# Counting tokens per expert on TensorE straight from the comparison, with the running total on GpSimd and, in the last three steps, on VectorE

## The reference

```python
_, top_group_idx = jax.lax.top_k(group_scores, n_top_groups)        # 4 of 8 groups
top_scores, top_idx = jax.lax.top_k(masked, K)                      # K = 4 of 32 experts
capacity = max(1, int(N / E * K * CAP_FACTOR))                      # 640 slots per expert
onehot = jax.nn.one_hot(flat_e, E, dtype=jnp.int32)
pos = jnp.cumsum(onehot, axis=0)[jnp.arange(N * K), flat_e] - 1     # place in the expert's queue
keep = pos < capacity
buf = jnp.zeros((E + 1, capacity, d), xf.dtype).at[e_s, p_s].set(xf[tok])[:E]
```

## Time and profile before

| | us |
|---|---|
| three runs | 600.43, 603.52, 605.98 |
| median | 603.52 |
| profiled execution, its time | 604.68 |
| its span in the profile | 602.5 |

### The profile page before, as it was taken

How to read it: one execution, slowest core, us unless ns; L and a number is a source line. 1 busy time by engine, 2 the same in 40 slices (tenths; PEclk the granted TensorE clock), 3 DMA queues, 4 the chain that set the end, 5 groups by cost and what they waited for, 6 DMA issues and landing times.

```text
span 602.5 us, 20827 instructions
## 1 busy us (share of the span) xinstructions
PE 513.2 (85%) x7427; PEld 423.3 (70%) x7427; DVE 424.7 (70%) x1297; ACT 323.1 (54%) x832; POOL 343.0 (57%) x362
## 2 busy tenths in 40 slices
PE   3558997989988798887669889999989999999756
PEld 2336665766666566665545589999989999998544
DVE  5666799779999899966676366756666676664264
ACT  3336775767777677655546225455446555454200
POOL 8520113276666566655777507777777777777600
PEclk9659998989999999977899979999999999999977
DMA  7889998887877665520000134543534554541198
GB/s 254 234 234 249 250 248 235 225 268 212 240 231 208 210 209 151 137 66 25 21 12 10 36 99 140 150 123 108 164 119 140 171 155 149 170 118 49 24 394 292
DMA packets 79417, 98.33 MB, mean 163 GB/s; under 512 B 12097, under 2 KB 59999, under 8 KB 79216
## 3 DMA queue, kind: packets, MB, share of 16 engines
q1 hardware_dynamic: 65280, 82.92, 47.2%
q0 software_dynamic: 9216, 12.02, 6.4%
q10 hardware_dynamic: 4848, 2.40, 1.4%
HBM read 50.00 MB, written 54.30 MB: 173 GB/s over the span
## 4 chain that ended last, share of the span: by engine, by line
PE 38%; DVE 6%; DMA 5%; issue 4%; POOL 3%; ACT 2%; SPq 0%; POOLq 0%; DVEq 0%; ACTq 0%
PE banks L1115 18%; PE banks L1141 12%; DMA rload<-pair_results 3%; PE banks L1126 3%; POOL expert_slots L490 2%; DVE mx L1239 1%; PE banks L932 1%; DMA pair_results<-yout,yidx 1%; PE banks L1050 1%; POOL pair_results L618 1%; PE banks L1167 0%; DMA xg<-expert_slots 0%; SPq L440 0%; PE banks L874 0%; ACT yout L805 0%
## 5 line engine op out<-in xcount | busy, mean ns | idle before, releaser
L618 POOL DMA_INDIRECT pair_results<-yout,yidx x160 | 159.3, 996 | 67.0 <-issue 38.1
L490 POOL DMA_INDIRECT expert_slots<-xfe,sidx x128 | 127.8, 998 | 89.7 <-issue 38.9
L1115 PE MATMUL banks<-xgT_parts,wgu_parts 128*128 128x320 f32 x768 | 131.3, 320 | 1.9 <-DVE hact L1506 1.7
L1115 PEld LDWEIGHTS banks<-xgT_parts,wgu_parts 128*128 128x128 f32 x768 | 113.9, 190 | 4.6 <-DVE hact L1506 2.3
L1239 DVE TENSOR_REDUCE mx<-banks 128x8 f32<-128x1024 f32 x64 | 78.0, 1219 | 21.0 <-PE banks L882 21.0
L1506 DVE TENSOR_TENSOR hact<-hact,banks 128x320 f32<-128x320 f32 x128 | 56.6, 482 | 43.0 <-ACT hact L786 42.1
L805 ACT ACTIVATE yout<-banks,ypair 128x128 f32<-128x128 f32 x160 | 44.8, 372 | 76.2 <-PE banks L1141 73.8
L655 ACT ACTIVATE pt<-banks 128x512 f32<-128x512 f32 x128 | 69.3, 593 | 27.9 <-PE banks L913 26.6
L1141 PE MATMUL banks<-wdn,hact 128*128 128x128 f32 x640 | 76.6, 275 | 1.1 <-DVE hact L1506 1.1
L1141 PEld LDWEIGHTS banks<-wdn,hact 128*128 128x128 f32 x640 | 75.0, 192 | 1.3 <-issue 1.3
L786 ACT ACTIVATE hact<-banks 128x320 f32<-128x320 f32 x128 | 53.5, 452 | 33.1 <-PE banks L1115 31.4
(11 more groups left out here) (154 smaller groups left out, 945.5 us busy)
## 6 DMA issues: line engine op xcount, KB each, us to landing
expert_slots<-xg SPq DMA_DIRECT2D x32, 325.0 KB, 4.8
xg<-expert_slots SPq DMA_DIRECT2D x32, 325.0 KB
pair_results<-zero SPq DMA_DIRECT2D x32, 256.0 KB
rload<-pair_results SPq DMA_DIRECT2D x16, 512.0 KB, 8.9
kS<-rotated_keys SPq DMA_DIRECT2D x32, 240.0 KB
qS<-rotated_queries SPq DMA_DIRECT2D x32, 192.0 KB
wgu<-in_L_ffn_wg_dram SPq DMA_DIRECT2D x32, 128.0 KB
wgu<-in_L_ffn_wu_dram SPq DMA_DIRECT2D x32, 128.0 KB
```

The costliest lines, as they stand in the source:

```text
L490: g.indirect_dma_start(out=slots_d, out_offset=bass.IndirectOffsetOnAxis(ap=sidx[:, m % NB, j, k:k + 1], axis=0), in_=xfe[:, m % NB, j, k, ...
L618: g.indirect_dma_start(out=pairs_d, out_offset=bass.IndirectOffsetOnAxis(ap=yidx[:, c, j:j + 1], axis=0), in_=yout[:, c, j, :], in_offset= ...
L1115: last = mm(bank[2 + 2 * w + h][:, 0:CH], wgu_parts[:, e.b, wp, w, h * P:(h + 1) * P], xgT_parts[:, e.b, xp, ch * CH:(ch + 1) * CH], start ...
```

## The change

`oh` becomes bf16, and PE takes it as it stands: one product with `before_b` per choice (four), the product with the running total, and one with `ones_b` per choice for tile 0 (four): nine products for three. DVE's reduce L1387 goes. PE and POOL now wait for the comparison itself (`route`, 16 r + 16). POOL's `counted()` makes the sum over choices and tiles from `oh` in three adds (128, 64 and 32 numbers per partition) and then adds the total, so four instructions for two. For the last three windows (LAST = 3, r = 13, 14, 15; steps without p) POOL does nothing of this, and DVE does it with a reduce and an add right behind the comparison. Since `oh` has one buffer that PE and POOL now read too, DVE's comparison waits until the products of window r - 1 are done (`pos_done`) and POOL's first add of window r - 1 is (`marks_added`).

```diff
@@ tiles
-        oh = sb("oh", [P, 2, TOPK, NE])
+        oh = sb("oh", [P, 2, TOPK, NE], BF16)
+        oh2 = sb("oh2", [P, TOPK, NE])
+        oh3 = sb("oh3", [P, 2, NE])
-        marks = sb("marks", [P, 2, 3, NE], BF16)
+        sofar = sb("sofar", [P, 2, NE], BF16)
@@ GpSimd
                 def counted():
-                    pool.wait_ge(S.sel_ready, r + 1)
+                    pool.wait_ge(S.route, 16 * r + 16)
...
-                    g.tensor_tensor(sum2[:, :], m[:, 1], m[:, 2], ALU.add).then_inc(S.marks_added, 1)
-                    pool.wait_ge(S.marks_added, r + 1)
+                    g.tensor_tensor(oh2[:, :, :], oh[:, 0], oh[:, 1], ALU.add).then_inc(S.marks_added, 1)
+                    pool.wait_ge(S.marks_added, 3 * r + 1)
+                    g.tensor_tensor(oh3[:, :, :], oh2[:, 0:2], oh2[:, 2:TOPK], ALU.add).then_inc(S.marks_added, 1)
+                    pool.wait_ge(S.marks_added, 3 * r + 2)
+                    g.tensor_tensor(sum2[:, :], oh3[:, 0], oh3[:, 1], ALU.add).then_inc(S.marks_added, 1)
+                    pool.wait_ge(S.marks_added, 3 * r + 3)
                     wait(pool, S.pos_done, r)
-                    g.tensor_tensor(marks[:, 1 - r % 2, 0], m[:, 0], sum2[:, :], ALU.add).then_inc(S.acc_ready, 1)
+                    g.tensor_tensor(sofar[:, 1 - r % 2], sofar[:, r % 2], sum2[:, :], ALU.add).then_inc(S.acc_ready, 1)
@@ GpSimd, steps without p
                     dispatch(z, 1, 1)
-                    if r is not None:
-                        counted()
                     for k in range(2, TOPK):
@@ TensorE
-                    pe.wait_ge(S.sel_ready, z + 1)
+                    pe.wait_ge(S.route, 16 * z + 16)
...
-                    mm(both, before_b[:, :], m[:, 1:3], start=True, stop=False, skip_group_check=True)
-                    mm(both, ones_b[:, :], m[:, 0:1].broadcast_to([P, 2, NE]), start=False, stop=False,
+                    for k in range(TOPK):
+                        mm(both, before_b[:, :], oh[:, :, k], start=(k == 0), stop=False, skip_group_check=True)
+                    mm(both, ones_b[:, :], sofar[:, z % 2].unsqueeze(1).broadcast_to([P, 2, NE]), start=False, stop=False,
                        skip_group_check=True)
-                    mm(both[:, 1], ones_b[:, :], m[:, 1], start=False, stop=True, skip_group_check=True)\
-                      .then_inc(S.pos_done, 1)
+                    for k in range(TOPK):
+                        last = mm(both[:, 1], ones_b[:, :], oh[:, 0, k], start=False, stop=(k == TOPK - 1),
+                                  skip_group_check=True)
+                    last.then_inc(S.pos_done, 1)
@@ VectorE
                 def mark():
                     dve.wait_ge(S.route, 16 * r + 14)
+                    wait(dve, S.pos_done, r)
+                    wait(dve, S.marks_added, 3 * r - 2 if r <= NP - LAST else 0)
...
+                def counted():
                     dve.wait_ge(S.route, 16 * r + 16)
-                    wait(dve, S.pos_done, r - 1)
-                    wait(dve, S.acc_ready, r - 1)
-                    with nc.allow_low_precision("zeros and ones"):
-                        v.tensor_reduce(marks[:, r % 2, 1:3], oh[:, :, :, :].rearrange("p j k e -> p j e k"), AX.X,
-                                        ALU.add).then_inc(S.sel_ready, 1)
+                    dve.wait_ge(S.acc_ready, r)
+                    v.tensor_reduce(sum2[:, :], oh[:, :, :, :].rearrange("p j k e -> p e (j k)"), AX.X, ALU.add)\
+                     .then_inc(S.marks_added, 1)
+                    dve.wait_ge(S.marks_added, 3 * (NP - LAST) + (r - NP + LAST + 1))
+                    wait(dve, S.pos_done, r)
+                    v.tensor_tensor(sofar[:, 1 - r % 2], sofar[:, r % 2], sum2[:, :], ALU.add).then_inc(S.acc_ready, 1)
...
                 at(r, mark)
+                if r is not None and p is None:
+                    counted()
```

5 lines of the change are left out of this document (2 added, 3 removed).

## The result

| | runs | median us | lowest to highest |
|---|---|---|---|
| before | 12 | 602.19 | 598.65 to 609.32 |
| changed | 12 | 598.05 | 590.75 to 602.14 |

The ratio is 0.9886, 95% interval 0.9849 to 0.9923, a gain of 1.1%. All ratios in this document leave out slow runs, those over 1.5% above the fastest run of their kernel (five of the changed kernel's twelve), while the medians of the table are of all runs and stand only 0.7% apart. The forecast was 597.0 us, worked out from a median before of 603.52 us; over twelve runs the median before is 602.19, so the two medians differ by 4.1 us where the forecast had 6.5.

The account below looks back on a forecast made before the run. DVE was taken to set the full steps and POOL's queue the experts' start. The terms, -4.6 + 0.9 - 0.6 - 2.3 = -6.6 us, gave 597.0 us from a median of 603.52, range 593.0 to 602.0.

Parts of the forecast that it names:

- What bounds the kernel: DVE, back to back, sets the full step; POOL's queue sets the experts' start; the expert stage shifts as a block.
- Term 1: Full steps: without DVE's reduce the maxima start 0.51 us sooner per step, for windows 3 to 11, 4.6 us.
- rival B: More than the sum: PE's clock stays up in the two steps or the 1.8 us stall is absent; 594, chance 0.12.
- Term 2: PE's nine counting products for three: 0.2 us more per step, hidden in PE's waits of 1.2 us.
- Rival A: Only the tail gains: PE takes over the full steps or two steps keep their length; 601.5, chance 0.15.
- Term 3: POOL's four adds for two: 0.9 us more per step, hidden in the full steps, +0.9 us in window 12.
- Terms 4 and 5: Tail: POOL starts window 12's adds sooner, -0.6 us; no POOL adds in windows 13, 14, 15, -2.3 us.
- The sum: Whole kernel: -4.6 + 0.9 - 0.6 - 2.3 = -6.6 us, giving 597.0 us.
- Rivals C and D: C: POOL's adds become the limit, 599.5, chance 0.09. D: PE's low clock in full steps, slower, 618, chance 0.04.
- What is late next: Before the experts: the slots' load still ends last, and PE's wait for it shrinks from 3.3 to under 2 us.

Follow-up runs that it names:

- the kernel with a DVE step of 16.06 us: Changed kernel with LAST = 16: DVE counts by a reduce and an add in every window, POOL makes no adds; 600.86 us, ratio 0.9984 to the kernel before.

## Why the prediction was right, and where by luck

**What bounds the kernel: right.** DVE sets the full step (its step is 0.80 us longer with 0.77 us more work and 0.55 shorter with the reduce gone), POOL's queue the tail, and the experts shifted as a block (the rest differs by 0.4 us here; over all profiles it lies between 251.0 and 257.9 us, which the change doesn't explain).

**Term 1, the reduce: mechanism right, its 0.51 us per step too high.** The step shrank from 15.81 to 15.26 us where L1333 took 0.20 us, by 0.55, but to 15.48 where L1333 and L1411 were both held up, by 0.33. That is two and three of the seven steps; the last two, 15.69 and 15.83 us for 16.09 and 15.88, gained 0.40 and 0.05. Without the step that had the stall the mean is 0.38 us, seven times that 2.7 us for 3.6. The rows add up: from the comparison to the maxima it is 0.34 us for 0.97, so 0.63 us were won, and 0.05 of it was lost at L1333 in the short steps, 0.21 and 0.07 at L1333 and L1411 in the others. The step that failed is that the prediction put POOL's adds at "in the full steps this hides" and asked only whether POOL had the time, not whether DVE works as fast beside them. L1333 went from 0.15 to 0.36 us and L1411 from 0.42 to 0.49, and DVE has no idle time in which this could vanish. DVE's own list says so in one line, and the experiment without adds and the one with adds later confirm it. The stretch still came to -4.48, because the 1.8 us stall of one step was gone in the changed kernel's profile. In PE of the kernel before, in order of time, it looks so:

```profile
199.75 0.25 PE L882 MATMUL banks<-kS,qS 64*64 64x128 bf16 x3 [1.91 <-issue]
```

PE stood there and waited for nothing that the profile shows. All three profiles of before have this in the same step (1.91, 1.33 and 1.71 us), and none of the eleven others has it there, though at least three of them have an idle time of 1.1 to 1.8 us of the same kind in an earlier step. That is a part of rival B, and its cause stays open.

**Term 1 in the two steps from 253 us: right, and hidden under the clock.** It was put at 0.51 us each; at equal clock it measured 0.44 and 0.32. The rest of the -4.44 us is the clock. With no low clock two steps take 29.7 us, with 3.4 us of it 30.6 to 31.2 (32.4 with a DVE step of 16.06 us), with 13.6 us 34.3: so 13.6 us at the low level cost 4.6. Before had 13.6, 10.2 and 13.6 us in three profiles; the changed kernel 3.4, 13.6 and 3.4, and its near relatives anything from 0 to 13.6. The low clock became rarer with the change in these few profiles, but it did not go; rival B named it ("if the clock stays up in the two steps") with a price of 1.85 us each, which is right, and gave all of B 0.12. It happened in two of three profiles. Whether the shorter waits of PE are the reason isn't settled: the kernel with six more products had 3.4 and 0 us of it in the two steps, but the kernel with a DVE step of 16.06 us had 3.4 us too.

**Term 2, the products: right.** Forecast 0.2 us per step, nowhere on the path; measured 0.029 us per product in the full steps, six 0.17, and six more again lengthened no step. Rival A's reason, PE as the limit, is out.

**Term 3, the adds' durations: right.** 0.436, 0.322 and 0.254 us against 0.45, 0.32 and 0.25. The Trainium skill (GPSIMD Engine Reference, Elementwise — side-by-side cycle accounting) has 2.6 cycles per element for a two-input add; from 32 to 128 numbers the trace adds 0.18 us, 1.9 ns per number or 2.3 cycles at the 1.2 GHz that the Trainium skill gives for GpSimd (same page, Specifications), so the trace agrees roughly. The Trainium skill (GPSIMD Engine Reference, Specifications) also says that GpSimd's interfaces to the on-chip memory are shared with VectorE, and that VectorE instructions with two inputs from there are among those that contend. L1333 and L1411 are such instructions, and the trace agrees: 0.21 and 0.07 us in a step. The section gives no price, so it would have named the loss before the forecast, but not its size.

**Terms 4 and 5, the tail: right behind steps at the low clock, handed back behind steps at the high one.** With the low clock before it, the tail gained 1.63 us for 2.0 forecast, and with POOL's adds put back it lost 4.75. But "all in the queue that sets the end" is true only as long as POOL waits for nobody. In the five profiles with the power in its old place and DVE counting only in the tail that had 3.4 us of low clock or none in the two steps before, the other engines came to the tail sooner than POOL's queue of dispatches let its power through; DVE waited 2.0 to 2.7 us for the power, PE fell idle for 2.6 to 3.3 us, the clock fell, and POOL then waited 2.3 to 3.1 us for ACT's copy of window 14. The step that failed is the sentence that DVE's waits in the tail only hide costs: nobody asked what happens when DVE waits for something that POOL has queued behind its own dispatches. Over three profiles the tail's gain was 0.15 us instead of 2.0.

**The sum.** Forecast -3.6, -1.0, -2.0. Measured means -3.8, -2.4, -0.15. The -3.8 is not term 1 as forecast either: 2.7 us is the reduce, the rest the stall. The two steps gave 1.4 us more than term 1 had, by the clock, and the tail 1.85 us less: these two are coupled, since the tail's new wait stands in just those profiles in which the two steps before kept the high clock for the most part. Ahead of all this, where the prediction put 0, the changed kernel's profiles lost 2.0 us on the mean. So that the forecast of 597.0 stands 1.0 us from the 598.05 measured is partly a right reading and partly luck: the errors had opposite signs, and the median it started from, 603.52, lay above the 602.19 of twelve runs.

**Rivals C and D** did not come: in the full steps no wait of DVE ended on POOL, and their clock stayed at 1.00. D's top price (+16.7 us) counted nine steps, though two of the nine already ran at the low clock in the earlier trace rows; seven steps by 1.85 are 13 us.

**What is late next: right in kind.** The load of the slots still ends last; PE's wait for it shrank from 3.3 to 3.5 us in the profiles of before to 2.60 to 2.73, not under 2.

**The spread.** The comparison of window 3 stood anywhere from 137.5 to 143.5 us, whatever the kernel. A part of this stands ahead of it, in the wait of the earlier trace rows: DVE gets that power anywhere from 122.6 to 128.4 us. Another part, 13.8 to 17.8 us from there to the comparison, has no cause that the profiles were asked for. With the clock in the two steps and the rest behind them, this moves a run by several us either way, so that ratios of 0.9878 and 0.9928 can belong to one kernel, and a microsecond in the tail can be read in profiles but not in six runs.

**Left open:** a version without any counting adds, which would price POOL's part by itself, wasn't tried; nor was one that holds PE's clock fixed, so the link between waits and clock rests on fourteen profiles. The stall ahead of L882, the lost 2 us ahead of the comparison of window 3 and the lower time with six more products have no cause shown.

## What to carry to other kernels

When work leaves a saturated DVE for POOL, price it twice: POOL's time, and what DVE's own two-input instructions lose beside it (0.2 us of a hoped 0.5 here). In an in-order queue that sets the end, look for a result that others need and that stands behind the queue's own long items: moving it forward (here POOL's power ahead of its dispatches) removed a wait of 3 us that no duration in the queue showed. And read a stretch's difference only beside its granted clock, in several profiles: here the clock made 3.7 of 4.4 us.

## What the runs showed of the hardware

- A two-number DVE instruction beside a POOL add of 128 numbers takes 0.36 us instead of 0.15 (never over 0.160 in 16 windows without adds); a 256-number one with two inputs, where it meets POOL's adds, 0.49 to 0.57 instead of 0.42.
- Products of bf16 with 64 or 32 columns follow each other in 0.028 to 0.038 us with the weight load of each: six of them took 0.17 us of PE in a full step, and the DVE reduce that they replace 0.59.
- In an idle time of 3.3 us in the tail PE's granted clock fell to 0.50, and its two products of 512 columns behind it took 1.92 us; after one of 0.5 us, at a clock of 1.00, they took 1.04.
- The changed kernel's two steps ran with anything from 3.4 to 13.6 us at the lower clock level, worth up to 3.7 us, with the same instructions in the same order.
